# Four neighbouring tokens per partition in a two-layer pair kernel: 512-byte runs to and from memory

## The chip, the core and the metric

The kernel runs on one core of one Trainium2 chip. The metric is device time in microseconds (us) of one execution. The kernel before takes 113.91 us, the median of three runs (113.77 to 114.04).

## The reference

The input x holds 128 x 128 tokens of 32 channels in fp32 (2 MB); a token is named by s and r. Two layers follow each other.

```
# layer 0
xn    = layernorm(x) * ln1_w + ln1_b                     # over the 32 channels
left  = sigmoid(xn @ left1)  * (xn @ left2)
right = sigmoid(xn @ right1) * (xn @ right2)
p     = einsum('nsre,nkre->nske', left, right)           # sum over r, for each of 32 features e
p     = layernorm(p) * ln2_w + ln2_b
q     = einsum('nrse,ez->nsrz', p, out_w) * sigmoid(xn @ gate)
x1    = x + q
# layer 1
l     = x1 @ W_left + b_left + x1 @ W_eq + b_eq
rsum  = sum over r of (x1 @ W_right + b_right)           # one per s and channel
o     = (l * rsum * sigmoid(x1 @ W_gate + b_gate)) @ W_out + b_out
out   = layernorm(o + x1) * ln_scale + ln_bias
```

All 11 matrices are 32 x 32. The output has the shape of x.

## The kernel before, in words

The program has one instruction list per engine, written out by hand; engines meet at semaphores, and an engine does its list strictly in order. There is no planner: the order of the calls in each engine's block is the schedule.

**Tiling.** A partition holds one r; along the free side lie the 128 values of s with their 32 channels (`x_tok`, 128 x 128 x 32). The work is cut into eight chunks of 16 values of s (`CHUNKS`, `SPC`), each 128 x 512 words. In memory x is ordered s, r, channel, so a partition's piece of one s is a run of 128 bytes, in and out. Loads are issued from SP's queue (L250), in two DMAs per group; ACT's queue takes half of the first group (L398), then the weights, replicated to four groups of 32 partitions (L399), and the two vectors of the last norm (L401). `SUMS1` lists the groups of loads: two halves of chunk 0, then seven chunks.

**Start and layer 0.** For each group VectorE computes the statistics of x as it arrives (`statistics1`, L581), ScalarE the roots (`root1_of`, L410), VectorE the reciprocals (`inverse1`, L588). GpSimd subtracts the mean (`centre`, L281) and scales (`normalise1`, L288) into `xc`; VectorE does that for the first half chunk itself (L608, L613). GpSimd's first step that needs the weights is the block of `lr_blk` (L299). TensorE transposes `xc` (`transpose_xn`, L802), four 128 x 128 pieces per chunk, ScalarE applies the affine step on the way out of PSUM (`affine1`, L421), and TensorE projects onto left and right (`project_lr`, L817), half a chunk at a time. ScalarE takes the sigmoid (`sigmoid_lr`, L431), and VectorE multiplies (`multiply_lr`, L596) and writes the result into `lr` with s innermost, feature by feature: neighbouring words of one token are written 512 bytes apart. The order on VectorE is: statistics of the first groups, then the products of chunk 0 between the later statistics, then the reciprocals that belong to chunks 3 and up, then the other products.

**Triangle.** Once all 16 products are there, TensorE multiplies left and right for each of the 32 features (L871); ScalarE copies the result to `p_sb`.

**The loop.** From about 50 us a software-pipelined loop goes over the chunks (`for i in range(CHUNKS + 2)` and the like on each engine): statistics and scaling of p (`statistics2`, `normalise2`, L352), transposes of p and of x (`transpose_t` L912, `transpose_x` L895, which reads `x_tok`), projection and gate, residual (`residual0`, L688 and L697), layer 1 with GpSimd's subtraction `low1` and product `times_right` (L368), the last projection, square, variance and norm. VectorE scales and GpSimd adds the bias into `sq` (`bias3`, L376); the last chunk's halves are added by VectorE (L785).

**Stores.** SP's queue stores each chunk from `sq` when it is final (L255), the last half chunk at L258; ACT's queue stores the half before it (L558). Each store has runs of 128 bytes.

Of the kernel before, what the change touches and what calls it, by code (L numbers as in the profile page):

```python
# [48 lines left out]
SUMS1 = [(0, 8), (8, 16)] + [(16 * n, 16 * n + 16) for n in range(1, 8)]  # L49
ROOTS1 = [(0, 8), (8, 16), (16, 32), (32, 48), (48, 64), (64, 96), (96, 128)]  # L50
TURNS = [(0, 8), (8, 16)] + [(16 * n, 16 * n + 16) for n in range(1, 8)]
OWN_CENTRE = 1
# [19 lines left out]
def place(tokens, lo, hi):  # L72

    rest = tokens.rearrange("p (m q) c -> p m q c", q=SPC // 2)
    if hi - lo < SPC:
        c, h = lo // SPC, lo % SPC // (SPC // 2)
        return rest[:, 2 * c:2 * c + 2, GRP * h:GRP * h + GRP]
    return rest[:, 2 * lo // SPC:2 * hi // SPC]


def arrived(b):

    lo, hi = SUMS1[b]
    return 32 * max(1, (hi - lo) // SPC)


# [5 lines left out]
def pair_layers(nc, x, weights, rows, out):  # L92
# [3 lines left out]
    x_tok_dram = x[0].rearrange("s r c -> r s c")  # L96
    out_tok_dram = out[0].rearrange("s r c -> r s c")
    n_w = weights.shape[1]

    with ExitStack() as ctx:  # L100
# [12 lines left out]
        pair_mask = sb("pair_mask", [P, 2, CH])  # L113
        lr_blk = sb("lr_blk", [P, 2, 4, CH])
# [22 lines left out]
        xc = sb("xc", [P, P, CH])  # L137
# [16 lines left out]
        t_tok = sb("t_tok", [P, 2, SPC, CH])  # L154
# [12 lines left out]

        bank = ctx.enter_context(nc.psum_tensor("bank", [P, 8, COLS], fp32))
# [10 lines left out]
        w_in, r_in, x_out = sem("w_in"), sem("r_in"), sem("x_out")  # L179
# [31 lines left out]
        def halves(cols, lo, hi):  # L211

            v = cols.rearrange("p (n h k) -> p n (h k)", n=2, h=2)
            if hi - lo == SPC:
                return v
            h = lo % SPC // (SPC // 2)
            return v[:, :, h * P:(h + 1) * P]

        def even_first(features):

            return features.rearrange("p e (q n) -> p n q e", n=2)

# [20 lines left out]
        @block.sync  # L243
        def _(sp):
            for b, (lo, hi) in enumerate(SUMS1):
                for first in range(lo, hi, SPC):
                    last = min(first + SPC, hi)

                    for n in range(2 if b else 1):
                        sp.dma_start(place(x_tok[:], first, last)[:, n], x_tok_dram[:, first + n:last:2, :]  # L250
                                     ).then_inc(x_in[b], 16)
            for c in range(CHUNKS - 1):
                s = slice(c * SPC, (c + 1) * SPC)
                sp.wait_ge(final, c + 1)
                sp.dma_start(out_tok_dram[:, s, :], sq[:, s, :]).then_inc(x_out, 16)  # L255
            s = slice(P - SPC // 2, P)
            sp.wait_ge(last_half, 2)
            sp.dma_start(out_tok_dram[:, s, :], sq[:, s, :]).then_inc(x_out, 16)  # L258
            sp.wait_ge(x_out, 16 * CHUNKS)

        @block.gpsimd
        def _(pool):
# [11 lines left out]
            for g in range(GRP):  # L274
                pool.wait_ge(consts, 1 + GRP + g)
                nc.gpsimd.memset(pair_mask[g * CH:(g + 1) * CH, g % 2, :], 1.0).then_inc(consts, 1)

            def centre(b):
                lo, hi = SUMS1[b]
                pool.wait_ge(stats1_ready, b + 1)  # L280
                nc.gpsimd.tensor_tensor(place(xc[:], lo, hi), place(x_tok[:], lo, hi), mean_of(lo, hi),  # L281
                                        ALU.subtract).then_inc(centred1_pool, 1)

            def normalise1(n):
                lo, hi = TURNS[n]
                pool.wait_ge(rstd1, holding(ROOTS1, lo) + 1)
                pool.wait_ge(centred1_pool, holding(SUMS1, lo) + 1 - OWN_CENTRE)
                nc.gpsimd.tensor_tensor(place(xc[:], lo, hi), place(xc[:], lo, hi),  # L288
                                        each_feature(rstd[:, 0], lo, hi), ALU.mult).then_inc(xn_pool, 1)

            def block_diagonal(dst, src):
# [4 lines left out]
            pool.wait_ge(consts, 1 + 2 * GRP)  # L296
            pool.wait_ge(w_in, 16)

            nc.gpsimd.tensor_tensor(lr_blk[:],  # L299
                                    w_rep[:, 0:4 * CH].rearrange("p (a m c) -> p a m c", a=1, m=4)  # L300
                                    .to_broadcast([P, 2, 4, CH]),
                                    pair_mask[:].rearrange("p g (a c) -> p g a c", a=1).to_broadcast([P, 2, 4, CH]),
                                    ALU.mult).then_inc(lr_blk_ready, 1)
            centre(1)
# [42 lines left out]
            def normalise2(c):  # L347
                s = slice(c * SPC, (c + 1) * SPC)
# [3 lines left out]
                nc.gpsimd.tensor_tensor(place(t_tok[:, c % 2], 0, SPC), even_first(p_sb[:, :, s]),  # L352
                                        even_first(rstd[:, 1:2, s]).to_broadcast([P, 2, SPC // 2, CH]),
# [686 lines left out]
```

## Time and profile before

| what | before |
|---|---|
| median of three runs | 113.91 us |
| span of the profiled execution | 112.1 us |
| the time beside that span (median less span) | 1.8 us |
| TensorE busy | 92.5 us, 83% |
| VectorE busy | 77.3 us, 69% |
| ScalarE busy | 66.6 us, 59% |
| GpSimd busy | 62.6 us, 56% |
| packets of the DMA queues | 33,486, of them 33,348 under 512 B |

The profiler gives the span from the first to the last event of one execution. Busy shares are averages over stages with different limits, so each stage is read by itself. A matmul in fp32 stands as two records. The DMA share is the mean over 16 engines, and it can be above 1, since reading and writing overlap.

### The profile page before, as it was taken

How to read it: one execution, taken by the hardware profiler on the slowest of the kernel's cores; microseconds unless marked ns; L12 is line 12 of the kernel's file. 1: busy time of each engine (PE TensorE's matmuls, PEld its weight loads, DVE VectorE, ACT ScalarE, POOL GpSimd, SP SyncE). 2: the span in 40 equal slices, each digit the busy share in tenths (PEclk: the TensorE clock that was granted, in tenths of full speed). 3: DMA queues.
4: the chain of work that ended last, by engine and by line, in shares of the span. 5: the costliest groups of instructions: out<-in, count | busy, mean ns of one | idle time of the engine just before them, and what ended most of it. 6: DMA issues, size and time to landing. Idle time of an engine off the chain costs nothing. (4 is left out here: it accounts for less than half of the span.)

```text
span 112.1 us, 1886 instructions
## 1 busy us (share of the span) xinstructions
PE 92.5 (83%) x600; PEld 72.3 (64%) x600; DVE 77.3 (69%) x284; ACT 66.6 (59%) x110; POOL 62.6 (56%) x78
## 2 busy tenths in 40 slices
PE   1997599789999899999979999999999996495000
PEld 1994368567776799545445789878877994394000
DVE  1528697986769800599975869699979963996500
ACT  0614888687785166795499463993797399330000
POOL 5037974599950040025488585587865492699400
PEclk9999999999999999999999999999999999999955
DMA  3669997000000000000000000000023006029996
GB/s 60 126 111 171 146 146 75 0 0 0 0 0 9 0 0 0 0 0 3 0 0 0 3 6 0 0 0 6 0 35 59 0 0 94 0 34 144 147 144 100
DMA packets 33486, 4.54 MB, mean 40 GB/s; under 512 B 33348, under 2 KB 33476, under 8 KB 33476
## 3 DMA queue, kind: packets, MB, share of 16 engines
q1 hardware_dynamic: 31632, 4.00, 27.6%
q10 hardware_dynamic: 1844, 0.41, 1.8%
q8 instruction: 5, 0.08, 0.3%
q14 instruction: 5, 0.04, 0.1%
HBM read 2.31 MB, written 2.10 MB: 39 GB/s over the span
## 5 line engine op out<-in xcount | busy, mean ns | idle before, releaser
L596 DVE TENSOR_TENSOR lr<-bank,sig_lr 128x512 f32<-128x512 f32 x16 | 15.9, 1044 | 3.7 <-ACT sig_lr L431 3.7
L817 PE MATMUL bank<-lr_blk,xnT 64*128 64x256 f32 x128 | 16.5, 392 | 1.0 <-ACT xnT L421 0.7
L352 POOL TENSOR_TENSOR t_tok<-p_sb,rstd 128x512 f32<-128x512 f32 x7 | 10.2, 1462 | 11.8 <-DVE rstd L666 11.8
L360 POOL TENSOR_TENSOR x_low<-x1T,x_high 128x512 fp32r<-128x512 f32 x8 | 10.3, 1290 | 7.5 <-ACT x_high L501 7.5
L817 PEld LDWEIGHTS bank<-lr_blk,xnT 64*128 64x128 f32 x128 | 11.8, 186 | 4.0 <-issue 2.3
L660 DVE BATCH_NORM_STATS2 stats<-p_sb 128x6 f32<-128x64 f32 x64 | 8.5, 211 | 7.0 <-ACT p_sb L465 7.0
L368 POOL TENSOR_TENSOR oT<-o_a,rsum 128x512 f32<-128x512 f32 x8 | 8.7, 1089 | 6.4 <-DVE o_a L706 4.2
L431 ACT ACTIVATE sig_lr<-bank 128x512 f32<-128x512 f32 x16 | 9.6, 598 | 3.9 <-PE bank L817 3.9
L581 DVE BATCH_NORM_STATS2 stats<-x_tok 128x6 f32<-128x64 f32 x64 | 8.9, 213 | 3.5 <-DMA x_tok<-in_x 3.3
L978 PEld LDWEIGHTS bank<-wout_blk,oT 128*128 128x128 f32 x64 | 8.1, 191 | 4.0 <-POOL oT L368 3.2
L978 PE MATMUL bank<-wout_blk,oT 128*128 128x128 f32 x64 | 8.8, 281 | 2.2 <-POOL oT L368 2.2
L501 ACT ACTIVATE x_high<-x1T 128x512 fp32r<-128x512 f32 x8 | 5.0, 628 | 8.5 <-DVE x1T L697 8.4
L376 POOL TENSOR_TENSOR sq<-lr,row_rep 128x512 f32<-128x512 f32 x7 | 9.8, 1420 | 0.0
L697 DVE SCALAR_TENSOR_TENSOR x1T<-bank,w_rep,u 128x128 f32<-128x128 f32 x32 | 9.3, 347 | 0.2
L967 PE MATMUL bank<-centre_blk,x1T 128*128 128x128 f32 x64 | 8.9, 282 | 0.6 <-DVE lr L724 0.5
L288 POOL TENSOR_TENSOR xc<-xc,rstd 128x512 f32<-128x512 f32 (+1 forms) x8 | 7.9, 995 | 2.3 <-DVE rstd L588 1.9
L281 POOL TENSOR_TENSOR xc<-x_tok,stats 128x512 f32<-128x512 f32 (+1 forms) x8 | 8.1, 1012 | 1.9 <-DVE stats L581 1.8
L706 DVE SCALAR_TENSOR_TENSOR o_a<-bank,leq_bias,sig 128x512 f32<-128x512 f32 x8 | 6.0, 744 | 3.5 <-ACT sig L507 3.2
L967 PEld LDWEIGHTS bank<-centre_blk,x1T 128*128 128x128 f32 x64 | 7.8, 192 | 0.9 <-DVE lr L724 0.7
L923 PE MATMUL bank<-tT,out_blk 128*128 128x512 f32 x16 | 8.3, 598 | 0.0
L871 PE MATMUL bank<-lr 128*128 128x128 f32 x64 | 7.4, 277 | 0.5 <-DVE lr L596 0.5
L410 ACT ACT_TABLE_LOAD x6 | 7.7, 1283 | 0.1
(104 smaller groups left out, 199.8 us busy)
## 6 DMA issues: line engine op xcount, KB each, us to landing
x_tok<-in_x SPq DMA_DIRECT2D x14, 128.0 KB, 4.2
out<-sq SPq DMA_DIRECT2D x7, 256.0 KB, 3.4
x_tok<-in_x SPq DMA_DIRECT2D x3, 64.0 KB, 2.7
w_rep<-in_weights ACTq DMA_DIRECT2D x1, 180.5 KB
out<-sq ACTq DMA_DIRECT2D x1, 128.0 KB, 3.7
out<-sq SPq DMA_DIRECT2D x1, 128.0 KB, 3.8
x_tok<-in_x ACTq DMA_DIRECT2D x1, 64.0 KB, 2.7
row_rep<-in_rows ACTq DMA_DIRECT2D x1, 32.0 KB, 5.1
```

The source lines that it names most:

```text
L352: nc.gpsimd.tensor_tensor(place(t_tok[:, c % 2], 0, SPC), even_first(p_sb[:, :, s]), even_first(rstd[:, 1:2, s]).to_broadcast([P, 2, SPC / ...
L360: nc.gpsimd.tensor_tensor(x1_low[:, c % 2], x1T[:, c % 3], x1_high[:, c % 2], ALU.subtract).then_inc(x1_low_ready, 1)
L368: nc.gpsimd.tensor_tensor(oT[:, c % 2].rearrange("p (b k) -> p b k", b=BLK), o_a[:, c % 2].rearrange("p (b k) -> p b k", b=BLK), rsum[:, c ...
L376: nc.gpsimd.tensor_tensor(sq[:, s, :], yn[:, s, :], row_rep[:, 1:2, :].to_broadcast([P, SPC, CH]), ALU.add).then_inc(final, 1)
L431: nc.scalar.activation(sig_lr[:, j % 3].rearrange("p (s f) -> p s f", f=2 * CH), src[:, :, 0:2 * CH], ACT.Sigmoid).then_inc(lr_sig, 1)
L581: last = nc.vector.bn_stats(stats1[:, k:k + 2, :].rearrange("p s v -> p (s v)"), x_tok[:, k:k + 2, :].rearrange("p s c -> p c s"))
L596: nc.vector.tensor_tensor(lr[:, :, s].rearrange("p f s -> p s f"), src[:, :, 2 * CH:4 * CH], sig_lr[:, j % 3].rearrange("p (s f) -> p s f" ...
L660: last = nc.vector.bn_stats(stats2[:, k:k + 2, :].rearrange("p s v -> p (s v)"), p_sb[:, :, k:k + 2])
L697: nc.vector.scalar_tensor_tensor(out=x1T[:, c % 3, b], in0=bank[:, XT, b], scalar=vec("b_out"), in1=u[:, c % 2, b], op0=ALU.add, op1=ALU.a ...
L817: last = nc.tensor.matmul(dst, xnT[half, c, k * P:(k + 1) * P], lr_blk[half].rearrange("p g m c -> p g (m c)"), start=True, stop=True, ski ...
L967: nc.tensor.matmul(in_order(bank[:, b], j), x1T[:, c % 3, k], centre_blk[:], start=j == 0, stop=False, skip_group_check=True)
L978: last = nc.tensor.matmul(in_order(bank[:, b], j), oT[:, c % 2, k], wout_blk[:], start=False, stop=j == BLK - 1, skip_group_check=True)
```

## The change

A partition now holds four neighbouring r (`RM` = 4) of every fourth s: the index of the partition is (b, q) with s = 16k + 4t + b and r = 4q + m, where k is the chunk and t one of four slots. The run of a partition in memory is the four r times 32 channels, 512 bytes, in loads and stores alike. The number of tokens per partition and chunk stays 16.

- A group is one DMA on SP's queue; ACT's queue no longer loads x.
- GpSimd writes `xc` with m outermost, so that a transpose takes the 128 words of one m, and its result is spread into the bank in runs of 32 words, which puts r in the order (m, q) behind it. `TURNS` is gone: chunk 0 is transposed whole and needs both halves, VectorE's and GpSimd's.
- The first root covers both halves of chunk 0 (`ROOTS1` has six entries instead of seven). On GpSimd the centring of the second half stands ahead of the wait for the weights; on ScalarE the root of chunk 1 stands behind the affine step of chunk 0.
- `lr_blk` has the two tokens of a pair innermost, the bank has the same order, and `multiply_lr` writes two neighbouring words at a time, in two instructions of 256 words each instead of one of 512.
- x is loaded a second time, into `sq`, with m outermost, in runs of 128 bytes, by eight DMAs behind the first load on SP's queue; `transpose_x` reads this copy and waits for all of it.
- The order of s in `lr`, `p_sb` and the norms is (b, k, t); the strides of `statistics2`, `root2_of`, `inverse2`, `normalise2`, `residual0`, `times_right` and the output of the last projection follow.

```diff
-ROOTS1 = [(0, 8), (8, 16), (16, 32), (32, 48), (48, 64), (64, 96), (96, 128)]
-TURNS = [(0, 8), (8, 16)] + [(16 * n, 16 * n + 16) for n in range(1, 8)]
+ROOTS1 = [(0, 16), (16, 32), (32, 48), (48, 64), (64, 96), (96, 128)]
...
-    x_tok_dram = x[0].rearrange("s r c -> r s c")
-    out_tok_dram = out[0].rearrange("s r c -> r s c")
+    def runs(dram):
+        return dram[0].rearrange("(k t b) (q m) c -> k (b q) t (m c)", k=CHUNKS, t=SLOTS, m=RM)
+    x_runs, out_runs = runs(x), runs(out)
+    x_by_m = x[0].rearrange("(k t b) (q m) c -> k (b q) m t c", k=CHUNKS, t=SLOTS, m=RM)
...
-        lr_blk = sb("lr_blk", [P, 2, 4, CH])
+        lr_blk = sb("lr_blk", [P, 4 * CH, 2])
...
+        x_res = sq[:].rearrange("p s c -> p (s c)").rearrange("p (k m j) -> p k m j", k=CHUNKS, m=RM)
...
@@ SP
-                    for n in range(2 if b else 1):
-                        sp.dma_start(place(x_tok[:], first, last)[:, n], x_tok_dram[:, first + n:last:2, :]
-                                     ).then_inc(x_in[b], 16)
+                sp.dma_start(x_tok[:, lo:hi, :].rearrange("p (t m) c -> p t (m c)", m=RM), x_runs[c][:, t:t + n]
+                             ).then_inc(x_in[b], 16)
+            for c in range(CHUNKS):
+                sp.dma_start(x_res[:, c].rearrange("p m (t c) -> p m t c", t=SLOTS), x_by_m[c]).then_inc(x_again, 16)
...
@@ GpSimd
             pool.wait_ge(consts, 1 + 2 * GRP)
+            centre(1)
             pool.wait_ge(w_in, 16)
...
-            centre(1)
             normalise1(1)
...
@@ ScalarE
-            act.dma_start(place(x_tok[:], lo, hi)[:, 1], x_tok_dram[:, lo + 1:hi:2, :]).then_inc(x_in[0], 16)
...
             root1_of(0)
-            root1_of(1)
             act.wait_ge(w_in, 16)
             affine1(0)
+            root1_of(1)
             root1_of(2)
+            sigmoid_lr(0, 0)
             affine1(1)
-            root1_of(3)
-            sigmoid_lr(0, 0)
+            sigmoid_lr(0, 1)
             affine1(2)
...
@@ VectorE
-                nc.vector.tensor_tensor(lr[:, :, s].rearrange("p f s -> p s f"), src[:, :, 2 * CH:4 * CH],
-                                        sig_lr[:, j % 3].rearrange("p (s f) -> p s f", f=2 * CH),
-                                        ALU.mult).then_inc(lr_ready, 1)
+                dst = lr[:].rearrange("p f (n h k t g) -> p n h k t f g", n=2, h=2, k=CHUNKS, t=2)
+                src = bank[:, lo:lo + 2].rearrange("p t (n w f g) -> p n w t f g", n=2, w=2, g=2)
+                sig = sig_lr[:, j % 3].rearrange("p (t n f g) -> p n t f g", t=2, n=2, g=2)
+                for n in range(2):
+                    last = nc.vector.tensor_tensor(dst[:, n, h, c], src[:, n, 1], sig[:, n], ALU.mult)
+                last.then_inc(lr_ready, 1)
...
             statistics1(0)
+            statistics1(1)
...
@@ TensorE
+                by_m = bank[:, c % 2].rearrange("p (b m q) -> p m b q", b=BLK, m=RM)
+                for m in range(RM):
+                    last = nc.tensor.transpose(by_m[:, m], xc[:, c, m], ident[:])
...
+                    pe.wait_ge(x_again, 16 * CHUNKS)
+                for m in range(RM):
+                    last = nc.tensor.transpose(bank[:, XT, m * P:(m + 1) * P], x_res[:, c, m], ident[:])
```

## Rows read from the trace of the kernel before

**Rows 1.** Timeline of SP's queue: start us, us, what; with the number of issues

```profile
103.55 4.29 SPq L255 DMA_DIRECT2D out<-sq  x2
...
107.89 1.10 SPq L258 DMA_DIRECT2D out<-sq  x1
```

**Rows 2.** Stores at L255, then the landing of L255 and L258: min, median, max

```profile
L255 SPq DMA_DIRECT2D out<-sq x7: 372/388/2706, 82.5 to 105.1; - x7
...
DMA to landing us min/median/max: 3.2/3.4/5.7
...
DMA to landing us min/median/max: 3.8/3.8/3.8
```

**Rows 3.** Windows (us): PE, PEld, DVE, ACT, POOL busy, PEclk, DMA share, GB/s

```profile
101.00:101.50 0.50, 0.50 (x7) 0.50 (x6) 0.50 (x2) 0.00 (x0) 0.50 (x2) 1.00 0.96 146
...
110.50:111.00 0.50, 0.00 (x0) 0.00 (x0) 0.00 (x0) 0.00 (x0) 0.00 (x0) 0.50 0.96 145
```

**Rows 4.** Timeline of the end: start us, us, engine, line, operation, count

```profile
97.68 7.25 POOL L376 TENSOR_TENSOR sq<-lr,row_rep 128x512 f32<-128x512 f32 x5
...
103.73 1.48 DVE L785 TENSOR_TENSOR sq<-lr,row_rep 128x256 f32<-128x256 f32 x1
```

**Rows 5.** Timeline of the start, same columns, in brackets the idle time before

```profile
0.74 0.51 ACTq L398 DMA_DIRECT2D x_tok<-in_x  x1
...
1.28 1.11 ACTq L399 DMA_DIRECT2D w_rep<-in_weights  x1
...
7.29 0.73 POOL L299 TENSOR_TENSOR lr_blk<-w_rep,pair_mask 128x256 f32<-128x256 f32 x1 [4.20 <-DMA w_rep<-in_weights]
...
7.36 0.61 DVE L581 BATCH_NORM_STATS2 stats<-x_tok 128x6 f32<-128x64 f32 x4 [1.96 <-DMA x_tok<-in_x]
...
11.59 0.32 ACT L410 ACTIVATE std<-stats,eps 128x16 f32<-128x16 f32 x1 [0.58 <-DVE stats L581]
...
18.38 2.14 DVE L581 BATCH_NORM_STATS2 stats<-x_tok 128x6 f32<-128x64 f32 x16 [0.63 <-DMA x_tok<-in_x]
...
20.76 1.05 POOL L288 TENSOR_TENSOR xc<-xc,rstd 128x512 f32<-128x512 f32 x1 [1.86 <-DVE rstd L588]
```

**Rows 6.** Loads of x issued from 1.2 to 1.8 us: duration ns, landing us

```profile
L250 SPq DMA_DIRECT2D x_tok<-in_x x2: 497/498/499, 1.2 to 1.8; - x2
...
DMA to landing us min/median/max: 2.7/4.1/5.6
```

**Rows 7.** Timeline of layer 0, the triangle's first load, and x transposed

```profile
26.41 0.65 PE L802 MATMUL bank<-ident,xc 128*128 128x128 f32 x4
...
26.99 2.00 PE L817 MATMUL bank<-lr_blk,xnT 64*128 64x256 f32 x16
...
28.92 0.66 PE L802 MATMUL bank<-ident,xc 128*128 128x128 f32 x4
...
36.82 1.02 DVE L596 TENSOR_TENSOR lr<-bank,sig_lr 128x512 f32<-128x512 f32 x1 [0.18 <-ACT sig_lr L431]
...
37.89 7.22 PEld L871 LDWEIGHTS bank<-lr 128*128 128x128 f32 x64 [0.62 <-DVE lr L596]
...
48.58 0.60 PE L895 MATMUL bank<-ident,x_tok 128*128 128x128 f32 x4
```

**Rows 8.** Groups by line and form: shapes, count, busy us, mean ns, idle before

```profile
L596 DVE TENSOR_TENSOR lr<-bank,sig_lr 128x512 f32<-128x512 f32 x16 | 15.9, 1044 | 3.7 <-ACT sig_lr L431 3.7
...
L739 DVE TENSOR_TENSOR lr<-bank,rstd 128x256 f32<-128x256 f32 x2 | 0.8, 424 | 0.9 <-PE bank L987 0.9
...
L421 ACT ACTIVATE xnT<-bank,w_rep 128x512 f32<-128x512 f32 x7 | 5.4, 777 | 0.4 <-PE bank L802 0.4
...
L288 POOL TENSOR_TENSOR xc<-xc,rstd 128x256 f32<-128x256 f32 x1 | 0.6, 617 | 0.1
```

**Rows 9.** DMA queue of ACT: packets, MB, share of 16 engines

```profile
q10 hardware_dynamic: 1844, 0.41, 1.8%
```

**Rows 10.** Window of 0.5 us in the load's plateau, columns as in rows 3

```profile
14.00:14.50 0.50, 0.24 (x2) 0.24 (x3) 0.50 (x1) 0.50 (x2) 0.50 (x2) 1.00 1.61 144
```

More of the change, by code:

```diff
@@ L43 @@
 ROWS = ["ln_scale", "ln_bias"]
-SUMS1 = [(0, 8), (8, 16)] + [(16 * n, 16 * n + 16) for n in range(1, 8)]
-ROOTS1 = [(0, 8), (8, 16), (16, 32), (32, 48), (48, 64), (64, 96), (96, 128)]
-TURNS = [(0, 8), (8, 16)] + [(16 * n, 16 * n + 16) for n in range(1, 8)]
-OWN_CENTRE = 1
+RM = 4
+SLOTS = SPC // RM
+HALF = SPC // 2
+SUMS1 = [(0, HALF), (HALF, SPC)] + [(16 * n, 16 * n + 16) for n in range(1, 8)]
+ROOTS1 = [(0, 16), (16, 32), (32, 48), (48, 64), (64, 96), (96, 128)]
+OWN = 1
 WARM_UP = 10
@@ L482, in root2_of @@
                 act.wait_ge(stats2_ready, last)
-                root(1, first * SPC, last * SPC, root2)
+                root(1, first, last, root2)
             gate0(0)
@@ L575, in statistics1 @@
                 lo, hi = SUMS1[b]
-                dve.wait_ge(x_in[b], arrived(b))
-                c, half = lo // SPC * SPC, hi - lo < SPC
-                first = lo % SPC // (SPC // 2) * GRP
-                places = [c + 8 * n + first + k for n in range(2) for k in (0, 2)] if half else range(lo, hi, 2)
-                for k in places:
+                dve.wait_ge(x_in[b], 16)
+                for k in range(lo, hi, 2):
                     last = nc.vector.bn_stats(stats1[:, k:k + 2, :].rearrange("p s v -> p (s v)"),
@@ L658, in statistics2 @@
                     dve.wait_ge(p_ready, 8)
-                for k in range(c * SPC, (c + 1) * SPC, 2):
-                    last = nc.vector.bn_stats(stats2[:, k:k + 2, :].rearrange("p s v -> p (s v)"), p_sb[:, :, k:k + 2])
+                for b in range(BLK):
+                    for t in range(0, SLOTS, 2):
+                        k = (b * CHUNKS + c) * SLOTS + t
+                        last = nc.vector.bn_stats(stats2[:, k:k + 2, :].rearrange("p s v -> p (s v)"),
+                                                  p_sb[:, :, k:k + 2])
                 last.then_inc(stats2_ready, 1)
             def inverse2(b):
-                s = slice(ROOTS2[b][0] * SPC, ROOTS2[b][1] * SPC)
                 dve.wait_ge(root2, b + 1)
-                nc.vector.reciprocal(rstd[:, 1, s], std[:, 1, s]).then_inc(rstd2, 1)
+                nc.vector.reciprocal(of_chunks(rstd[:, 1], *ROOTS2[b]), of_chunks(std[:, 1], *ROOTS2[b])
+                                     ).then_inc(rstd2, 1)
             statistics2(0)
```

238 lines of the change are left out of this document (104 added, 134 removed).

## The prediction

> **What bounds the kernel now.** I read the end first, then the start, then the middle.
>
> The end. The timeline of SP's queue shows stores issued up to 107.89 us [rows 1]. Issuing one costs 0.37 to 0.39 us when nothing is queued, but the last two full ones took 4.29 together from 103.55, the longer of them 2.71 [rows 1, 2]. Their landing went from 3.2 us undisturbed to 5.7 [rows 2]. The windows say why: from 101 to 111 us the store runs at about 145 GB/s with the engines' busy share near 0.95, one flat plateau of 20 half microseconds [rows 3]. The compute behind it had long ended: GpSimd's last additions at 97.68 + 7.25 = 104.93, VectorE's last half chunk at 103.73 + 1.48 = 105.21 [rows 4]. The last store is issued at 107.89, lands at 107.89 + 3.8 = 111.7 and the span ends at 112.1. So 6.5 us after the last arithmetic are the store of 128-byte runs, and the bound there is the DMA rate.
>
> The start. The timeline shows GpSimd waiting until 7.29 us for the weights and VectorE until 7.36 for the second half chunk of x [rows 5]. These are one event: the two loads on SP's queue that begin at 1.2 and 1.8 us take 2.7 and 5.6 us to land, thus 3.9 and 7.4 [rows 6], and the second is issued while ACT's queue issues the weights (1.28 to 2.39) [rows 5]. After that VectorE, ScalarE and GpSimd work in a fixed order; x itself is late only once (the last 16 statistics wait 0.63 us). GpSimd can scale chunk 3 when those are done, at 20.76, and TensorE transposes it right behind that [rows 5].
>
> The middle. From about 24.5 us a chunk of layer 0 takes 2.51 us (transposes at 26.41 and 28.92), and TensorE has 0.65 + 2.0 us of work in it, overlapped: TensorE is the bound [rows 7]. VectorE's two products of 1.04 us fit [rows 7, 8]. Only the last product is exposed: 36.82 + 1.02 = 37.84, and the triangle's weights load at 37.89 [rows 7]. From there to 98 us the same work is done by the same instructions on other strides.
>
> **The change part by part.**
>
> *Stores in 512-byte runs.* Descriptors per full chunk fall from 2048 to 512. One 128-byte descriptor costs 0.96 x 16 x 0.5 us / (73 KB / 128 B) = 13.5 ns of an engine in the plateau [rows 3]. The trace has no 512-byte run. Bounds: at four times the descriptor time the rate stays 145 GB/s and nothing is won; at the same descriptor time it is 580 GB/s. The nearest row is ACT's queue, which holds the weights: 1.8% of 16 engines' 112.1 us is 32.3 us for 1844 packets [rows 9]. Take off 1024 stores at 13.5 ns and 512 loads at 13.5 to 23 ns (the upper from the load's plateau, 1.61 x 16 x 0.5 us / 562) [rows 3, 10], and 128 rows of 256 bytes at about twice the shortest (1.7 to 3 us): 4 to 10 us stay for the weights' 128 runs of 1444 bytes, 30 to 77 ns each. A straight line to 512 bytes gives 18 to 32 ns, 256 to 440 GB/s. I take the slow end, 256 GB/s, because a rounded share stands behind it; a chunk then needs 1.0 us instead of 1.8.
>
> Replay of the end: an undisturbed store lands in 3.2 us, of which 1.8 are data, so about 1.0 lies before the data and 0.4 behind. Chunk 5, issued 103.55: data 104.55 to 105.6; ACT's half to 106.1; chunk 6, free at 104.93 and no longer stuck in the issue, to 107.1; the last half, ready at 105.21, to 107.6, landing 108.0 instead of 111.7. That is -3.7 us. At 145 GB/s it is 0, at 440 it is -4.4.
>
> *Loads in 512-byte runs, one DMA per group.* What this removes is the wait of 0.63 us, and the load's share of the engines. It cannot pull the start forward by itself, since the order hangs on the weights (W, now 7.29). ACT no longer loads x first, so the weights are issued 0.54 us earlier (0.74 instead of 1.28). Against that, rows 6 read like turns taken one for one: the late 64 KB DMA has 512/16 = 32 descriptors per engine, and it ended with the weights. If W's load starts near 3.2 us, 4.1 us lie in it; with 32 turns on its engines a turn is 128 ns, and x's share grows from 14-23 to 18-40 ns, +0 to +0.8 us. So W moves by -0.54 to +0.3; I take -0.1. The second half chunk of x has 16 descriptors per engine now and comes ahead of W.
>
> *The new order at the start.* Chunk 0 is transposed whole, so it needs GpSimd's half, which stands behind the weights: W, block of weights 0.73, normalise 0.62 [rows 5, 8], transposes and hand-over 0.7, affine step 0.78 [rows 8], then the root of chunk 1, which moves behind that affine step, 0.3, its reciprocal 0.25, eight statistics 1.1 (half of 2.14 [rows 5]), with hand-overs W + 4.6 = 11.9 for the root of chunk 2, which starts at 11.59 now [rows 5]: +0.3. Queued behind that root are ACT's table load and first sigmoid, so VectorE's first product is 0.3 later; VectorE then runs without a gap (its two early products 0.24 shorter each, below; no DMA wait 0.63), and the last statistics end 0.47 earlier. With W's -0.1: **-0.5 us** at 20.76, which I carry to 36 us since TensorE is the bound between. Bounds +0.9 (W + 0.3, products no shorter) and -1.1 (W earlier by 0.54).
>
> *Products in pairs of words.* 16 instructions of 512 become 32 of 256. One of 512 that writes single words 512 bytes apart takes 1044 ns; one from PSUM that writes in order takes 424 ns for 256 [rows 8]. Two are thus 0.81 at best, back to back. If a pair cost what two single words do, the halves would be about 0.6 and the sum 1.15. I take 0.81 because the write is the only part that was slow: last product **-0.25 us** (bounds -0.3 and +0.15); the other fourteen in the TensorE-bound stage are worth nothing.
>
> The Trainium skill, "SBUF — State Buffer", on cachelines, says that a 16-byte line gives full bandwidth from two accesses on. By that a pair writes at full rate; the long single-word product agrees, and no run of this kernel shows a pair yet.
>
> *Second load of x (16,384 descriptors of 128 bytes).* At the load's 144 GB/s [rows 10] 2 MB are 14.5 us; behind the first load it ends by 25 to 30 us, and its first reader is the transposes at 48.58 [rows 7]: 0. It would cost only if it took longer than 35 us. Nothing else is on SP's queue until the first store.
>
> *Strides in the loop of 50 to 96 us* (transposes, residual, GpSimd products): runs of 32 words as now in other places; 0, bounds ±0.5.
>
> **Sum.** -3.7 - 0.5 - 0.25 = -4.45. The profiled span of 112.1 becomes 107.65; the median of 113.91 lies 1.8 above the span, which I keep: **109.5 us**.
>
> **Rivals.**
>
> 1. *The store is bound by bytes, not by descriptors.* For it: the load's plateau is 144 GB/s too, with quite another busy share (1.61 beside 0.96) [rows 3, 10]. Against it: the weights' packets. Then the end gives 0 to 1 us: 113.9 - 0.75 - 0.5 = 112.7.
>
> 2. *The weights come later.* If a turn on an engine lets several descriptors through, x's share in 4.1 us grows with the run: say it was 1.5 us of that and doubles. W moves +1.5 - 0.5 = +1, the whole start with it: 109.5 + 1.1 = 110.6; with a threefold share 112. Against it: the equal ends in rows 6. The Trainium skill, "DMA: Bandwidth & Descriptors" (Queues, rings and completion order), says an engine drains a whole packet of about 9 to 17 descriptors before it changes rings; by that rule this rival is the case.
>
> 3. *Slower: VectorE becomes the bound of layer 0.* If each half product keeps a long time (three dimensions on both sides, twice the instructions), fourteen products after 20.5 us are 28 instructions. They fit until 0.62 us each (17.3 us / 28); from 0.77 they eat the other 4.2 us; at 1.04, as now for the double size, they end at 20.5 + 29.1 = 49.6 instead of 37.8: 113.9 + 11.8 - 4 = 121.7. Against it: 424 ns for 256 [rows 8].
>
> 4. *More at the start and end:* W -0.54 and 440 GB/s: 109.5 - 0.7 - 0.6 = 108.2.
>
> **Numbers.** Forecast 0.62 (108.6 to 110.5), rival 1 0.12, rival 2 0.13, rival 3 0.06, rival 4 0.07. Leaving out rival 3 and the tails, the range is 108.0 to 112.0. Less than 0.2% (0.23 us, about what a measurement of this kernel can tell) only comes from rival 1 with a lost start: 0.03. Slower 0.06, faster 0.91.
>
> **What would show it.** Stores: issues of 0.4 us to the end, the last landing some 2.8 us after 105.2 less the shift, a rate well over 200 GB/s. Start: GpSimd's block of weights at about 7.2, chunk 3's scaling near 20.3, no DMA wait of VectorE after the first chunk. Products: near 0.4 us each, the triangle's first load some 0.75 us earlier than 37.89. Wrong would be a store rate of 150 GB/s, weights after 8 us, or gaps of TensorE that end on VectorE's products between 24 and 36 us.

## The result and the profile after

The changed kernel took 109.43 us (median of four, 108.84 to 110.06) beside 113.97 (113.77 to 114.50) before it: a ratio of 0.9586, 95% interval 0.9512 to 0.9661. A repeat on the day of the experiments (e1) gave 108.89 and 0.9568 [0.9517, 0.9619]. The forecast was 109.5, range 108.0 to 112.0. Executions more than 1.5% above the fastest of the same kernel are left out of every ratio. The profiled execution took 108.94 with a span of 107.1, so 1.8 us lie outside the span, as before.

The end first. The timeline of SP's queue, after:

```profile
98.18 5.73 SPq L254 DMA_DIRECT2D out<-sq  x5
...
104.34 0.37 SPq L260 DMA_DIRECT2D out<-sq  x1
```

The stores of the tail and their landing (KB each, median us from issue to landing), after:

```profile
out<-sq SPq DMA_DIRECT2D x5, 256.0 KB, 2.3
out<-sq ACTq DMA_DIRECT2D x1, 128.0 KB, 2.3
out<-sq SPq DMA_DIRECT2D x1, 128.0 KB, 2.4
```

Windows of the end, after (columns as in rows 3; the last two are DMA share and GB/s):

```profile
104.00:105.00 1.00, 0.00 (x0) 0.00 (x0) 0.31 (x1) 0.00 (x0) 0.00 (x0) 1.00 0.70 197
105.00:106.00 1.00, 0.00 (x0) 0.00 (x0) 0.00 (x0) 0.00 (x0) 0.00 (x0) 1.00 1.04 286
106.00:107.00 1.00, 0.00 (x0) 0.00 (x0) 0.00 (x0) 0.00 (x0) 0.00 (x0) 0.78 0.32 87
```

The last arithmetic, after: GpSimd's and VectorE's additions, and ahead of them the last `project_y` on TensorE:

```profile
96.44 7.07 POOL L376 TENSOR_TENSOR sq<-lr,row_rep 128x512 f32<-128x512 f32 x5
...
103.56 0.75 DVE L779 TENSOR_TENSOR sq<-lr,row_rep 128x256 f32<-128x256 f32 x2
...
96.53 2.08 PE L965 MATMUL bank<-wout_blk,oT 128*128 128x128 f32 x8 [1.59 <-POOL oT L369]
```

No store waits in the queue any more (0.37 us for the last issue, against 2.71 and 1.10 in [rows 1, 2]), a store lands in 2.3 to 2.6 us instead of 3.2 to 5.7, and the flat plateau of 145 GB/s [rows 3] has become single humps of up to 286. The last addition ends at 104.31, the span at 107.1: 2.8 us, against 6.9 before [rows 4]. The last `project_y` is late for another reason: it took 2.08 us, because the granted clock was 0.5 (the lower of TensorE's two levels) from 96.3 to 99.7 us, after TensorE had waited 1.59 us for GpSimd. In e1 the same wait was followed by no fall, and it took 1.16.

The start and layer 0, after (GpSimd, VectorE, ScalarE and the triangle's first load, from four timelines):

```profile
5.75 0.61 DVE L574 BATCH_NORM_STATS2 stats<-x_tok 128x6 f32<-128x64 f32 x4 [2.17 <-DMA x_tok<-in_x]
...
6.52 0.65 POOL L284 TENSOR_TENSOR xc<-x_tok,stats 128x256 f32<-128x256 f32 x1 [3.58 <-DVE stats L574]
7.13 0.61 POOL L303 TENSOR_TENSOR lr_blk<-w_rep,pair_mask 128x256 f32<-128x256 f32 x1
...
10.38 0.25 DVE L581 RECIPROCAL rstd<-std 128x16 f32<-128x16 f32 x1 [0.88 <-ACT std L409]
...
11.64 0.32 ACT L409 ACTIVATE std<-stats,eps 128x16 f32<-128x16 f32 x1 [1.29 <-DVE stats L574]
...
16.25 3.16 DVE L574 BATCH_NORM_STATS2 stats<-x_tok 128x6 f32<-128x64 f32 x24
...
18.12 1.28 ACT L409 ACT_TABLE_LOAD   x1
...
19.76 0.58 DVE L581 RECIPROCAL rstd<-std 128x16 f32<-128x16 f32 x2 [0.35 <-ACT std L409]
...
20.09 1.05 POOL L291 TENSOR_TENSOR xc<-xc,rstd 128x512 f32<-128x512 f32 x1 [1.58 <-DVE rstd L581]
...
31.36 3.85 PE L806 MATMUL bank<-lr_blk,xnT 64*128 64x256 f32 x32
...
35.87 0.76 DVE L591 TENSOR_TENSOR lr<-bank,sig_lr 128x256 f32<-128x256 f32 x2 [0.22 <-ACT sig_lr L427]
...
36.68 5.43 PEld L860 LDWEIGHTS bank<-lr 128*128 128x128 f32 x48 [0.35 <-DVE lr L591]
```

The products as a group, after (count, busy us, mean ns):

```profile
L591 DVE TENSOR_TENSOR lr<-bank,sig_lr 128x256 f32<-128x256 f32 x32 | 12.0, 416 | 6.4 <-ACT sig_lr L427 5.9
```

GpSimd's block of weights is at 7.13 (7.29 before), now right behind its centring, which waited for the statistics of x's second half chunk, and not for the weights. The last statistics run 24 in a row without a DMA wait, chunk 3 is scaled at 20.09 (20.76) [rows 5], the last product takes 0.76 (1.02) and the triangle starts at 36.68 (37.89) [rows 7]. From there to the last `project_y` all stays: 96.53 against 97.77, -1.24 against -1.21. So the span's -5.0 is -1.24 up to there, +0.34 in the tail's slower clock, and -4.1 behind the last addition.

### The profile page after: what moved, and what is told of

The parts are those of the page before. It is cut to its first block and busy times, and to the rows that moved or that the text cites. A ratio compares the mean times of both kernels' runs of the same rounds, so it can differ in the third digit from the quotient of the medians.

```text
span 107.1 us, 1898 instructions
## 1 busy us (share of the span) xinstructions
PE 93.0 (87%) x600; PEld 73.1 (68%) x600; DVE 72.6 (68%) x299; ACT 65.6 (61%) x108; POOL 62.2 (58%) x78
## 5 line engine op out<-in xcount | busy, mean ns | idle before, releaser
L591 DVE TENSOR_TENSOR lr<-bank,sig_lr 128x256 f32<-128x256 f32 x32 | 12.0, 416 | 6.4 <-ACT sig_lr L427 5.9
L965 PE MATMUL bank<-wout_blk,oT 128*128 128x128 f32 x64 | 9.7, 300 | 2.2 <-POOL oT L369 2.2
L965 PEld LDWEIGHTS bank<-wout_blk,oT 128*128 128x128 f32 x64 | 8.9, 208 | 4.0 <-POOL oT L369 3.2
L418 ACT ACTIVATE xnT<-bank,w_rep 128x512 f32<-128x512 f32 x8 | 6.2, 776 | 4.3 <-PE bank L793 4.3
```

Source lines behind the costliest of these rows:

```text
L591: last = nc.vector.tensor_tensor(dst[:, n, h, c], src[:, n, 1], sig[:, n], ALU.mult)
L965: last = nc.tensor.matmul(spread(bank[:, b], j), oT[:, c % 2, k], wout_blk[:], start=False, stop=j == BLK - 1, skip_group_check=True)
```

## The experiments

This table is read from the timelines of the profiled executions, in us; W is the start of GpSimd's block of weights, "triangle" its first load, "p_y" the last `project_y`.

```
kernel                     W     chunk 3  triangle  p_y    last add  span
before                     7.29  20.76    37.89     97.77  105.21    112.1
e9  pairs, old address     7.32  20.82    37.41     97.29  105.09    111.6
e5  address alone          7.18  19.85    37.00     96.82  104.26    110.0
e4  pairs + address        6.62  18.85    35.43     95.32  103.21    108.1
e2  after, 128-byte stores 7.49  21.25    37.84     97.69  105.58    110.8
after                      7.13  20.09    36.68     96.53  104.31    107.1
e1  after again            7.49  20.45    37.03     96.90  104.34    107.3
e6  after, old address     6.96  20.45    37.03     96.88  104.64    107.5
e11 after, root first      7.27  19.81    36.39     96.26  103.70    106.6
e7  after, four loads      6.06  18.84    35.42     95.28  102.72    105.6
e3  after, words apart     7.92  21.67    38.80     98.67  106.40    109.3
e8  after, no second load  7.28  21.02    37.59     97.44  105.33    108.0
e10 after, fillers         7.79  21.84    38.42     98.76  105.87    108.9
e12 e7, e11 and fillers    6.04  19.54    36.12     96.45  103.56    106.6
```

**e1_after_again**: the changed kernel as it is.

> The changed kernel once more, beside which the other three of this job are read. Between its runs it has stood at 108.8 to 108.9 us and at 109.9 to 110.1, and the mean granted clock was lower in the slower ones (0.968 beside 0.981 and 0.995). Theory: the two values differ by the clock that TensorE has in the last 12 us, where the profiled run shows 0.50 from 96.5 to 99.8 us after 1.6 us without a matmul; then the values fall into the same two groups again and the slower has the lower clock. Rival: ordinary scatter; then values lie between 109.0 and 109.8 as well, and the clock does not go with them.

Measured 108.89 (108.67 to 110.04, six runs). Timelines of e1 at the end, to compare with those of after:

```profile
96.90 1.16 PE L965 MATMUL bank<-wout_blk,oT 128*128 128x128 f32 x8 [1.59 <-POOL oT L369]
...
96.81 7.25 POOL L376 TENSOR_TENSOR sq<-lr,row_rep 128x512 f32<-128x512 f32 x5
...
102.41 1.93 DVE L779 TENSOR_TENSOR sq<-lr,row_rep 128x256 f32<-128x256 f32 x2
```

Without the fall of the clock VectorE starts its last additions 1.15 us earlier and needs 1.93 instead of 0.75, while GpSimd adds beside it until 104.06. From the start of the last `project_y` to the end of the last addition the kernel before and e1 take 7.44 us, after 7.78: the fall cost it 0.34 us and not the 1.1 that lie between the two groups of times, so the theory falls as it stands. The times do go with the mean clock (108.67 to 109.05 at 0.993 to 0.996, 109.42 at 0.972, 110.04 at 0.967), and e8 shows where the rest is lost. W differs by 0.36 between two profiles of one kernel; differences of that size are read as scatter below.

**e2_stores_128**: final values laid out with the four tokens outermost, stores in 128-byte runs again.

```diff
-sp.dma_start(out_runs[c], sq[:, s, :].rearrange("p (t m) c -> p t (m c)", m=RM))
+sp.dma_start(out_by_m[c], by_m(sq[:], c * SPC, (c + 1) * SPC))
```

> The changed kernel, but its final tile has m outermost, so that every store goes out in runs of 128 bytes again; the output is the same. Theory: the end was won by the length of the store's runs. Then the store's plateau is near 145 GB/s, the last landing is again 6 us or more after the last addition (2.4 now), and the time rises by 3.5 to 4.2 us, to about 113. Rival: the end was won by the shorter issue on SP's queue and by the work before it ending earlier, while bytes bound the store; then the time stays within 1 us of 109.4.

Measured 111.65 (111.48 to 112.67), 2.8 above e1. Windows of e2's end:

```profile
105.00:106.00 1.00, 0.00 (x0) 0.00 (x0) 0.58 (x2) 0.00 (x0) 0.00 (x0) 1.00 1.61 174
106.00:107.00 1.00, 0.00 (x0) 0.00 (x0) 0.00 (x0) 0.00 (x0) 0.00 (x0) 1.00 1.59 174
```

The run length of the stores is the largest single part of the gain. But the plateau is 174 GB/s, not the 145 of [rows 3] with the same 128-byte runs. Something else had changed with them.

**e3_words_apart**: the two words of a pair 64 bytes apart (the output's tokens come in another order).

```diff
-dst = lr[:].rearrange("p f (n h k t g) -> p n h k t f g", ...)
+dst = lr[:].rearrange("p f (n h g k t) -> p n h k t f g", ...)
```

> The changed kernel, but the two words that a product writes one after the other lie 64 bytes apart (the order of s in lr is permuted, so the tokens of the output are permuted too); same number and size of instructions. Theory: products are faster because two words that follow each other share a line; then one product of 256 words takes 0.5 to 0.6 us instead of 0.42, the triangle's first load comes 0.3 to 0.6 us after that of the changed kernel (36.7), and the time rises by as much. Rival: the split into two instructions or the other order of reading made them faster; then 0.42 stays, and the time too.

Measured 111.18 (110.61 to 111.85), 2.3 above e1. The group of products in e3, and the four projections that end layer 0:

```profile
L591 DVE TENSOR_TENSOR lr<-bank,sig_lr 128x256 f32<-128x256 f32 x32 | 15.6, 595 | 3.9 <-ACT sig_lr L427 3.9
...
32.93 4.13 PE L806 MATMUL bank<-lr_blk,xnT 64*128 64x256 f32 x32
```

595 ns instead of 416, the last pair 1.03 instead of 0.76: what makes the products quick is the neighbourhood of the words, not the split of the instruction. Their price is more than that last pair. Behind W the triangle starts 1.33 us later than in after (30.88 against 29.55): 0.41 of it arises at the two early pairs, which stand between statistics, 0.28 in the last four projections (4.13 us, 3.85 in after) and 0.27 in the last pair, about 1.0 together; 0.28 was lost ahead of the first pair, where the clock fell to 0.50 near 10 us. The later W (7.92) and a fall of the clock in the tail are no price of the products.

**e4_before_pairs**: the kernel before with the pair products alone.

```diff
-pair_mask = sb("pair_mask", [P, 2, CH])
-lr_blk = sb("lr_blk", [P, 2, 4, CH])
+pair_mask = sb("pair_mask", [P, 2])
+lr_blk = sb("lr_blk", [P, 4 * CH, 2])
```

> The kernel before with this part of the change alone: the block of weights has the two tokens of a pair innermost, and each product is two instructions of 256 words that write two words 8 bytes apart one after the other. Loads, stores and order are those of before. Theory: two words within 16 bytes suffice; a product takes 0.42, the triangle's first load comes 0.25 to 0.55 us before 37.89 (0.25 for the last product, up to 0.3 where TensorE waited for the products before it), and the time falls by the same, if the stores at the end do not take it back. Rival: only words that touch are fast; then 0.5 to 0.6 for each, and the triangle no earlier or up to 0.15 us later.

Measured 110.17 (109.90 to 110.38), -3.8 us: far from what either theory gave. Here the words of a pair lie 8 bytes apart, and a product takes 415 ns, no more than for neighbouring words. Windows of e4's end:

```profile
103.00:104.00 1.00, 0.00 (x0) 0.00 (x0) 0.21 (x1) 0.00 (x0) 0.00 (x0) 1.00 1.60 173
104.00:105.00 1.00, 0.00 (x0) 0.00 (x0) 0.00 (x0) 0.00 (x0) 0.00 (x0) 1.00 1.64 174
```

The stores of this kernel are those of before, line for line, and yet move at 173 GB/s. What differs is where they read: `pair_mask` has shrunk from 256 bytes per partition to 8 (a slot of 32), so that all tensors behind it moved 224 bytes down. `x_tok` begins at byte 28256 in the kernel before (32 behind a multiple of 64) and at 28032 (a multiple of 128) in e4 and in the changed kernel; `xc` and `sq` follow it in steps of 16,384. The change does this too, and the prediction hadn't seen it.

**e5_before_aligned**: the kernel before and the address alone.

```diff
+pad = sb("pad", [P, 8])
 x_tok = sb("x_tok", [P, P, CH])
```

> The kernel before with 32 bytes per partition left unused ahead of x_tok, nothing else: x_tok, xc and sq begin at a multiple of 128 bytes (28288 for x_tok) instead of 32 behind a multiple of 64 (28256). Theory, SBUF address: the 128-byte runs of loads and stores then move at the rates of e4_before_pairs (load 164 to 196 GB/s instead of 144, store 172 to 175 at a busy share of 1.6 instead of 145 at 0.96), GpSimd's block of weights is at about 6.6 us instead of 7.3, chunk 3 is scaled 1.2 to 1.9 us earlier, and the last store is issued within 0.1 us of the last addition: 110.4 to 111.2 us, leaving 0.2 to 0.9 of e4's -3.85 to the products. Rival, products: the address does nothing, both rates stay at 145, 114.0 us, and e4's gain came from the products alone.

Measured 111.72 (four runs 111.46 to 111.84, two near 113.5), ratio 0.9802 [0.9783, 0.9821]: -2.25 us from 32 unused bytes. Windows of e5's end, then its timelines of VectorE and GpSimd at the start:

```profile
105.00:106.00 1.00, 0.00 (x0) 0.00 (x0) 0.00 (x0) 0.00 (x0) 0.00 (x0) 0.50 1.62 172
106.00:107.00 1.00, 0.00 (x0) 0.00 (x0) 0.00 (x0) 0.00 (x0) 0.00 (x0) 0.50 1.60 175
```

```profile
16.48 3.15 DVE L582 BATCH_NORM_STATS2 stats<-x_tok 128x6 f32<-128x64 f32 x24
...
19.85 1.05 POOL L289 TENSOR_TENSOR xc<-xc,rstd 128x512 f32<-128x512 f32 x1 [1.13 <-DVE rstd L589]
```

The store's rate is that of e4, the DMA wait of the last statistics (0.63 us in [rows 5]) is gone, chunk 3 comes 0.91 earlier and 5.7 us instead of 6.9 follow the last addition. W, forecast at 6.6, stayed at 7.18. The address is a cause of its own; its size was somewhat overestimated.

**e9_pairs_old_address**: e4 with the same 32 bytes, which put `x_tok` back to 32 behind a multiple of 64 (28064; the kernel before has 28256).

> e4_before_pairs (the kernel before with the pair products alone) with 32 bytes per partition left unused ahead of x_tok, so that x_tok, xc and sq begin at 32 behind a multiple of 64 again, as in the kernel before. Theory, two separate causes that add: the store and load plateaus are back at 145 GB/s, the pairs keep the 1.5 us that lie between e5 (111.7) and e4 (110.2): 112.1 to 112.8 us, with chunk 3's scaling some 0.5 us earlier than 20.76 and the triangle 1.0 to 1.2 earlier than 37.89. Rival, the prediction's sizes: 0.48 in the start and 0.25 for the last product, the rest of the layer nothing: 113.1 to 113.4 us. Second rival, the address gave e4 everything: 113.9 us.

Measured 113.44 (113.16 to 113.65, twelve runs), ratio 0.9948 [0.9924, 0.9972]: -0.5 us. The theory of two causes that add falls; the prediction's sizes come nearest. Timelines of VectorE, GpSimd and TensorE in e9 (the last row is the four projections that end layer 0):

```profile
18.45 2.14 DVE L582 BATCH_NORM_STATS2 stats<-x_tok 128x6 f32<-128x64 f32 x16 [1.24 <-DMA x_tok<-in_x]
...
20.82 1.05 POOL L289 TENSOR_TENSOR xc<-xc,rstd 128x512 f32<-128x512 f32 x1 [2.47 <-DVE rstd L589]
...
36.59 0.76 DVE L599 TENSOR_TENSOR lr<-bank,sig_lr 128x256 f32<-128x256 f32 x2 [0.22 <-ACT sig_lr L431]
...
32.08 3.85 PE L819 MATMUL bank<-lr_blk,xnT 64*128 64x256 f32 x32
```

The same four projections before, then a window of e9's store:

```profile
32.02 4.14 PE L817 MATMUL bank<-lr_blk,xnT 64*128 64x256 f32 x32
```

```profile
105.00:106.00 1.00, 0.00 (x0) 0.00 (x0) 0.09 (x1) 0.00 (x0) 0.00 (x0) 1.00 0.95 145
```

The store is back at 145 GB/s. VectorE finishes its two early products sooner and then waits for x, 1.24 us instead of 0.63: the gain of 0.6 becomes a longer wait, and chunk 3 is where it was. Only the end of the layer is left, 37.41 against 37.89: the last four projections take 3.85 us (4.14 before), and the last pair 0.76. So address alone is -2.25, pairs alone -0.5, both -3.8. The early products count only where x is not the bound, and x is freed from that by the address or, in the changed kernel, by the longer runs. Of the 1.05 that the two together give beyond their sum, the profiles of e5 and e4 have 0.44 in these products (chunk 3 earlier by 1.00, W by 0.56); the rest isn't told apart from the scatter of W.

**e6_after_shifted**: the changed kernel with the same `pad`, thus with `x_tok` at 28064, as in e9.

> The changed kernel with the same 32 bytes ahead of x_tok: its 512-byte runs now begin at 32 behind a multiple of 64, as the 128-byte runs of the kernel before did. Theory, short runs suffer most: a run of 512 bytes loses little by its address, the store's plateau is 250 to 290 GB/s and the time 108.9 to 109.6; then the run length by itself gives most of the end. Rival, the address costs every line the same share: the store falls from 290 by the 18% that e4 and before differ (175 to 145), to about 240 GB/s, with the second load at 145, and the time is 109.7 to 110.5.

Measured 109.63 (109.28 to 109.88), ratio 0.9626 [0.9604, 0.9648]. Windows of e6, its first loads and its last stores:

```profile
8.00:12.00 4.00, 3.53 (x18) 3.42 (x20) 2.34 (x17) 1.06 (x3) 2.39 (x3) 1.00 1.15 288
105.00:106.00 1.00, 0.00 (x0) 0.00 (x0) 0.00 (x0) 0.00 (x0) 0.00 (x0) 1.00 1.02 287
```

Runs of 512 bytes move as fast here (288 and 287) as in after (291 from 8 to 12 us, 286 at the end), and from chunk 3 on the table's rows of e6 and e1 agree to 0.3 us. Of the changed kernel's gain the address thus explains 0 to 0.7 us. The medians differ by 0.7 and the intervals barely overlap, but no stage of the profile shows a slower load or store. What it shows is TensorE at half pace from 8.5 to 11.5 us: the transposes of chunk 0 take 1.08 us (0.63 in after and e1) and the fillers behind them 2.21 (1.28), though the rows give a granted clock of 1.00 there. Chunk 3 lies 13.49 behind W, not 12.96, which uses up that W came 0.53 earlier than in e1. And at a mean clock of 0.967 to 0.972 e6 took 109.64 and 109.88, after and e1 109.42 to 110.06, so part of the 0.7 goes with the clock. e6 is the change without its accident: -4.3 us, where the prediction's sum was -4.45.

**e7_w16**: the weights in four DMAs of 32 partitions instead of one broadcast.

```diff
-act.dma_start(w_rep[:], weights.rearrange("(a p) n -> a p n", a=1).to_broadcast([GRP, CH, n_w])
-              ).then_inc(w_in, 16)
+for g in range(GRP):
+    act.dma_start(w_rep[g * CH:(g + 1) * CH, :], weights).then_inc(w_in, 16)
```

(and the waits for `w_in` at `16 * GRP`.)

> The changed kernel with the weights loaded by four DMAs of 32 partitions each instead of one broadcast DMA over 128 partitions: only the issue of that load changes. Theory, the weights set the start: they land 1 to 2 us earlier than 7.1, chunk 3's scaling and the triangle of layer 0 move by 0.8 to 1.5 us, 107.4 to 108.2 us. Rival, the second half chunk of x sets it: the issues cost ACT 1.1 us more, x's half still lands near 5.7, GpSimd's block moves by under 0.5 us and the time by -0.3 to +0.5.

Measured 107.75 (five runs 107.52 to 107.81, one 109.91), ratio 0.9464 [0.9448, 0.9479], faster than both kernels: 1.1 below e1. Timelines of e7, VectorE and GpSimd:

```profile
3.33 1.24 DVE L574 BATCH_NORM_STATS2 stats<-x_tok 128x6 f32<-128x64 f32 x8 [0.66 <-DMA x_tok<-in_x]
...
9.13 0.25 DVE L581 RECIPROCAL rstd<-std 128x16 f32<-128x16 f32 x1 [2.10 <-ACT std L409]
...
6.06 0.61 POOL L303 TENSOR_TENSOR lr_blk<-w_rep,pair_mask 128x256 f32<-128x256 f32 x1 [0.68 <-DMA w_rep<-in_weights]
```

W is 1.07 earlier than after's, and so, beyond what was expected, is the second half chunk of x: all eight statistics of chunk 0 run in a row from 3.33, where the second four waited until 5.75. GpSimd now waits for the weights again, 0.68 us. Chunk 3 and the triangle come 1.25 earlier. From 3 to 6 us, microsecond by microsecond, the DMA engines moved 113, 157 and 132 GB/s at a share of 0.51 to 0.70 in after, and 200, 290 and 296 at 0.85 to 1.06 in e7: they weren't full while x waited. That the one load of weights holds up the start is shown, and that it does so through x's second half chunk.

**e8_no_reload**: no second load; the residual reads `x_tok`.

> The changed kernel without its second load of x: the residual of layer 0 transposes x_tok as it lies, so it adds the tokens of a chunk in a permuted order (the residual's tokens are changed, nothing else). Prediction and theory: the second load is over by about 26 us and read first at 47.4, so its absence gives nothing, 108.7 to 109.1 us. Rival, it disturbs the first load or SBUF between 12 and 26 us: chunk 3's scaling and the triangle come 0.2 to 0.8 us earlier, 108.0 to 108.6 us.

Measured 109.96 (109.83 to 111.30), which neither theory gave. TensorE's timeline in e8, then windows of it:

```profile
8.79 0.96 PE L790 MATMUL bank<-ident,xc 128*128 128x128 f32 x4 [2.41 <-POOL xc L288]
```

```profile
8.00:9.00 1.00, 0.21 (x2) 0.24 (x3) 0.47 (x4) 0.00 (x0) 0.64 (x1) 0.97 1.07 315
9.00:10.00 1.00, 1.00 (x7) 1.00 (x6) 0.83 (x7) 0.15 (x1) 0.10 (x1) 0.50 0.98 276
```

After 2.41 us without work TensorE had the clock 0.50 until past 12 us, and chunk 3 came at 21.02. Three of the four runs had a mean clock of 0.966 to 0.968, as had the 110.0 runs of after and e1. This profile shows what such an execution loses: 0.78 us between W and chunk 3 (13.74, 12.96 in e1) and 0.45 between the last `project_y` and the last addition (7.89, 7.44 in e1), where the clock fell once more. Together that is the distance of the two groups of times, and 3.2 and 3.4 us at 0.50 lower the mean clock of the 108 us by 0.03. Up to the fall nothing is earlier than in after and e1 (W 7.28, second half of x 5.90), so no cost of the second load shows; the time itself can't settle a few tenths.

**e10_fills**: TensorE's pauses filled.

```diff
+fill(6, 14)
 transpose_xn(0)
...
+if i - 3 == CHUNKS - 1:
+    fill(TT, 10)
```

> The changed kernel with TensorE's pauses filled by products that nobody reads: 14 before the transposes of chunk 0 and 10 before the last project_y. Theory, the clock makes the two groups of the changed kernel's times (108.7 and 110.0): in e8 the granted clock was 0.50 from 8.8 to 12.4 us, after a TensorE pause of 2.4 us; with the pause filled no run is at 110.0, and all are at 108.5 to 109.0 with a mean clock over 0.99. Rival, the groups come from the landing of the weights or of x: one or two of six runs stay near 110, and the others gain nothing or lose up to 0.3 us to the fillers.

Measured 110.81 (110.65 to 111.00, four runs, mean clock 0.990 to 0.992). Timeline of TensorE in e10:

```profile
6.83 3.75 PE L821 MATMUL bank<-ident 128*128 128x128 f32 x28
10.42 0.60 PE L793 MATMUL bank<-ident,xc 128*128 128x128 f32 x4
```

A miss of sizing: a filler is two passes, 28 of them take 3.75 us, and the transposes of chunk 0 come at 10.42 instead of 8.64 (after) or 9.00 (e1). That is most of the 1.9 us. The times lie within 0.35 us, not in two groups; with four runs that hints at the clock and does not show it.

**e11_root_first**: one step of the new order taken back.

```diff
-affine1(0)
 root1_of(1)
+affine1(0)
```

> The changed kernel with one step of the new start order taken back: ScalarE takes the root of chunk 1 before the affine step of chunk 0, as the kernel before did, not behind it. Theory, that step is the new order's cost: VectorE's wait for that root (0.88 and 1.02 us in the two profiles) shrinks to 0.4, GpSimd scales chunk 1 and chunk 3 0.4 us earlier, first sigmoid 0.4 earlier, the affine step 0.4 later without harm: 108.3 to 108.7 us. Rival, the affine step and TensorE's first projection set what follows: they come 0.5 us later and the time is 109.0 to 109.4.

Median 109.18 of six, ratio 0.9500 [0.9439, 0.9562], which overlaps e1's; the times spread from 107.84 to 111.04. Timelines of e11:

```profile
10.07 0.25 DVE L581 RECIPROCAL rstd<-std 128x16 f32<-128x16 f32 x1 [0.44 <-ACT std L409]
...
19.81 1.05 POOL L291 TENSOR_TENSOR xc<-xc,rstd 128x512 f32<-128x512 f32 x1 [1.60 <-DVE rstd L581]
```

VectorE's wait falls to 0.44 and chunk 3 lies 12.54 behind W, where after and e1 have 12.96: the 0.4 us of the theory, in the trace. The time can't confirm it.

**e12_together**: e7, e11 and fillers (6 and 10).

> The changed kernel with e7's four weight loads, e11's order and fillers for TensorE (6 before the transposes of chunk 0, 10 before the last project_y). In e7 VectorE waited 2.10 us for the root of chunk 1. Theory, with the weights early this order is the next bound: that wait goes, chunk 3 is scaled 0.5 to 1.3 us earlier than e7's 18.84, and the time is 106.4 to 107.2 us. Rival, the arrival of x is the next bound: VectorE waits for x in chunks 2 to 7 instead, chunk 3 moves by under 0.3 us and the time is 107.4 to 107.8.

Measured 107.80 (106.85 to 108.38). Timelines of TensorE, VectorE and GpSimd in e12:

```profile
6.82 2.29 PE L821 MATMUL bank<-ident 128*128 128x128 f32 x12
8.94 0.60 PE L793 MATMUL bank<-ident,xc 128*128 128x128 f32 x4
...
7.94 0.25 DVE L581 RECIPROCAL rstd<-std 128x16 f32<-128x16 f32 x1 [0.44 <-ACT std L409]
...
19.54 1.05 POOL L291 TENSOR_TENSOR xc<-xc,rstd 128x512 f32<-128x512 f32 x1 [2.10 <-DVE rstd L581]
```

The reciprocal is 1.2 earlier than e7's, but the fillers push the transposes from 7.39 to 8.94, and chunk 3 is later than e7's 18.84. Neither theory is tested; what e7's loads with the old order of the root are worth stays open.

## Why the prediction was right, and where it was not

**Stores: -3.7 forecast, -4.1 in the profile.** The mechanism held: fewer descriptors, a higher rate, no store stuck in its issue. At the end a share of 1.04 of 16 engines moves 286 GB/s, so a 512-byte descriptor takes 1.04 x 16 us / (286 KB / 512 B) = 30 ns, inside the forecast's 18 to 32 and near its upper end, and the rate lies over the 256 GB/s that was taken. The replay was 0.4 too long behind the last issue: it lands in 2.4. Rival 1 (bound by bytes) is out: 286 is not 145. e2 gives back 2.8 us, not 4.1, its 128-byte runs moving at 174 GB/s and not at 145.

**Start: -0.5 forecast, -0.67 in after, -0.31 in e1 and e6.** The steps came as replayed: W 7.13 (about 7.2 forecast), the root of chunk 2 at 11.64 (11.9), no DMA wait at the last statistics. After and e1 differ in W alone: in both chunk 3 is scaled 12.96 us behind it, before 13.47, which is -0.51 where the forecast had -0.47. That these two agree is luck. The forecast's own terms (+0.3, two products 0.24 shorter each, a wait of 0.63 gone) add up to -0.81, not to -0.47, and behind W the last statistics do end 0.95 earlier (19.41 in after, 20.52 before). But then chunk 3's reciprocal waits 0.35 us for ScalarE's root, which stands behind a table load that ends at 19.40; before, these roots were done at 19.35 and VectorE came later. The forecast had no such wait. ScalarE's roots before:

```profile
18.80 0.55 ACT L410 ACTIVATE std<-stats,eps 128x16 f32<-128x16 f32 x2
```

What failed besides is the reason, "the order hangs on the weights": in all eight profiles with x in 512-byte runs and one load of weights, W lies 1.38 us behind the start of the statistics of x's second half chunk (5.75 and 7.13 in after, 5.58 and 6.96 in e6, 6.11 and 7.49 in e1), with no wait of GpSimd between. The forecast had that half chunk come ahead of W, and so it does, but it sets W. In [rows 5] both came at once.

Rival 2 (the weights a microsecond later) isn't seen: they had landed by W, so by 6.96 to 7.92, and W was 6.62 to 7.32 with x in 128-byte runs (before, e4, e5, e9). The rule of the Trainium skill, "DMA: Bandwidth & Descriptors" (Queues, rings and completion order), on whole packets of descriptors, taken as the prediction took it, would have W near 8.3; the latest of these profiles has 7.92, and none shows when weights that nobody waits for landed. That the two loads hold each other up is real all the same, only the other way round: e7 has x's half chunk 1.8 us earlier. The forecast's term for the root behind the affine step, +0.3, is borne out by e11's 0.4.

**Products: -0.25 for the last pair, measured 0.76 beside 1.02.** Rival 3 (VectorE the bound) is out at 416 ns, a third below its threshold of 0.62 us. What the Trainium skill, "SBUF — State Buffer" (cachelines), says of lines used twice agrees: pairs write at the pace of words in a row (416 beside the 424 of [rows 8], 415 with the words 8 bytes apart), pairs torn 64 bytes apart need 595. The step that failed is "the other fourteen in the TensorE-bound stage are worth nothing": TensorE was held by the long products after all. In e9, where the start is as before, the last four projections take 3.85 us instead of 4.14, and so they do in after and e1; in e3, which has after's order and banks but slow products, they take 4.13. With these 0.29 the triangle's shift adds up: 0.31 + 0.29 + 0.26 = 0.86 in e1, 0.67 + 0.29 + 0.26 = 1.22 in after, where the forecast had 0.75 and the table 0.86 and 1.21.

**Strides and second load: 0 forecast, no cost found.** From triangle to last `project_y` before takes 59.88 us, after 59.85. For the second load, which ends ahead of that, e8 shows no cost up to the fall of its clock and can't settle a few tenths.

**What the prediction did not see:** that the smaller `pair_mask` moves every later tensor. It left the total right, because runs of 512 bytes don't care (e6). Had the change kept its 128-byte runs, as e4 does, the forecast would have missed by three microseconds.

That the median came within 0.1 us of the forecast is in part luck as well. In the profiled execution the terms come to -4.1 - 0.67 - 0.29 - 0.26 + 0.34 = -5.0, half a microsecond more than the -4.45 forecast; two of the four executions, at a mean clock of 0.968, took about 1.1 us more than the other two, and that brought the median back.

## What to carry to other kernels

When a transfer in short runs is the bound, note the SBUF address of its tensor before pricing anything else, and pad it to a multiple of 128 bytes: here 32 bytes were worth 2.25 us. An edit that changes the size of a small tensor moves all that are allocated behind it, so a part tried alone needs the same addresses as the whole. And a gain on an engine that waits for a load behind it is worth nothing until the load is quicker (e9), so parts that are worth 0.5 and 2.25 alone can be worth 3.8 together.

## What the runs showed of the hardware

- Stores of 128-byte runs that begin in SBUF at 32 behind a multiple of 64 (28256 and 28064, thus 96 and 32 behind a multiple of 128) move at 145 GB/s, at a multiple of 128 at 172 to 175; loads from 12 to 16 us at 145 to 147 and at 179 to 180. For 512-byte runs 28064 and 28032 give 286 to 288. A multiple of 64 that is none of 128 wasn't tried.
- The busy share is no measure of how near a DMA plateau is to its limit: the store of 128-byte runs showed 0.95 at 145 GB/s and 1.6 at 173. The 0.95 in [rows 3] was read as such a limit.
- Two words 8 bytes apart are written as fast as neighbours (415 and 416 ns); 64 bytes apart they cost 595.
- One broadcast load of the weights holds up the loads of x beside it: in four loads, the second half chunk of x came by 3.9 us instead of 5.75. Why was not tried.
- VectorE's half-chunk addition takes 0.42 us when GpSimd is done (after), and the two of e1, while GpSimd adds, 0.53 and 1.48 (0.75 and 1.93 for the pair).
- TensorE's clock fell to 0.5 after the same pause of 1.59 us in one execution (after) and not in another (e1). A fall cost 0.34 us in the tail and, in e8, 0.78 at the start. In e6 TensorE ran at half pace for 3 us at a granted clock of 1.00 in the rows.
